# Both LayerNorms of a node unit moved to ScalarE, its steps placed at other points of the block loop, and another order of the node blocks

## What is computed

```python
msg = relu(h[src] + e) + 1e-7
m = msg * t
ex = exp(m - segment_max(m, dst)[dst])
alpha = ex / (segment_sum(ex, dst)[dst] + 1e-16)
agg = segment_sum(msg * alpha, dst)
z = relu(layernorm((h + agg) @ w1 + b1, g1, bb1))   # 128 wide
out = z @ w2 + b2
# from layer 1 on:  h = h + genconv(relu(layernorm(h, ln_g, ln_b)))   # 64 wide
```

## Time and profile before

| | |
|---|---|
| median of 3 runs | 5808.66 us (5808.57 to 5826.21) |
| the profiled execution | 5825.41 us, its span 5823.0 us |
| busy | PE 81%, DVE 78%, ACT 34%, POOL 69% of the span |
| mean granted TensorE clock | 0.868 of full speed |
| layers 0, 1, 2, 3 begin at (first gather) | 1686.0, 2708.5, 3732.3, 4757.7 us |

### The profile page before, as it was taken

One profiled execution on the slowest core, in us unless ns is written; L12 is line 12 of the kernel. 1 busy time (PEld: TensorE's weight loads), 2 busy tenths in 40 slices (PEclk: granted clock), 3 DMA queues, 4 the chain that ended last, 5 costly groups with the idle time before them and its releaser, 6 DMA issues.

```text
span 5823.0 us, 108077 instructions
## 1 busy us (share of the span) xinstructions
PE 4692.3 (81%) x43853; PEld 3246.1 (56%) x43853; DVE 4557.1 (78%) x8649; ACT 1992.2 (34%) x3506; POOL 4032.3 (69%) x3659
## 2 busy tenths in 40 slices
PE   6727788899958888886888798688888867896887
PEld 6726677788945554553555455355545544554544
DVE  9723555654549998996999899699989968997887
ACT  3314675665523332332233223223323322222222
POOL 2433777777637777774777777477777747777775
PEclk8966987976659999998999999899999978998988
DMA  8993777775665556554555655455565545555552
GB/s 338 413 304 111 274 282 270 263 274 211 240 218 196 183 198 181 186 200 144 181 186 200 174 192 193 148 173 198 191 174 200 184 148 177 188 189 161 177 178 96
DMA packets 317390, 1192.47 MB, mean 205 GB/s; under 512 B 139314, under 2 KB 142564, under 8 KB 249556
## 3 DMA queue, kind: packets, MB, share of 16 engines
q1 hardware_dynamic: 166676, 920.68, 42.9%
q0 software_dynamic: 128800, 209.18, 14.0%
q10 hardware_dynamic: 21408, 55.60, 2.4%
HBM read 930.35 MB, written 254.82 MB: 204 GB/s over the span
## 4 chain that ended last, share of the span: by engine, by line
DVE 35%; PE 13%; POOL 10%; issue 8%; DMA 2%; ACT 2%; SPq 0%; DVEq 0%; POOLq 0%
POOL gb L1285 9%; PE bank L1394 9%; DVE ep_layers L1384 5%; DVE xb L1318 5%; DVE ep_layers L1345 5%; DVE ep_layers L1370 4%; DVE ep_layers L1340 4%; PE bank L1302 2%; DMA gb<-ztab,ovi 2%; DVE xb L1328 1%; DVE ds L1404 1%; DVE na L1431 1%; ACT hb L282 1%; DVE st L254 1%; PE bank L1448 1%
## 5 line engine op out<-in xcount | busy, mean ns | idle before, releaser
L1285 POOL DMA_INDIRECT gb<-ztab,ovi x2512 | 2794.2, 1112 | 869.5 <-issue 736.3
L1394 PE MATMUL bank<-ep_layers,keep 128*128 128x512 f32 (+3 forms) x4928 | 2248.6, 616 | 43.2 <-DVE ep_layers L1384 43.2
L1394 PEld LDWEIGHTS bank<-ep_layers,keep 128*128 128x128 f32 x4928 | 995.9, 205 | 1241.1 <-issue 1181.8
L1302 PE MATMUL bank<-zpw,oh_layers 128*128 128x64 bf16 x28812 | 880.8, 194 | 104.2 <-DMA zpw<-ztab 104.1
L1302 PEld LDWEIGHTS bank<-zpw,oh_layers 128*128 128x128 bf16 x28812 | 874.4, 98 | 159.0 <-issue 137.1
L1131 POOL DMA_INDIRECT ecell<-zpw,ptg x588 | 627.3, 1067 | 227.8 <-issue 175.6
L1376 ACT ACTIVATE ep_layers<-ep_layers,pack 128x1280 f32<-128x1280 f32 (+14 forms) x484 | 641.9, 1347 | 190.1 <-DVE ep_layers L1370 183.9
L1370 DVE SCALAR_TENSOR_TENSOR ep_layers<-xb,bank 128x1280 f32<-128x1280 f32 (+14 forms) x484 | 689.2, 1468 | 6.8
L1384 DVE SCALAR_TENSOR_TENSOR ep_layers<-xb,ep_layers 128x1280 f32<-128x1280 f32 (+14 forms) x484 | 687.0, 1469 | 0.4
L960 PE MATMUL bank<-byk,zpw 96*102 96x102 f32 (+13 forms) x4608 | 624.3, 317 | 43.2 <-DVE zpw L941 39.4
L960 PEld LDWEIGHTS bank<-byk,zpw 96*102 96x102 f32 (+13 forms) x4608 | 609.4, 224 | 58.5 <-DVE zpw L941 49.2
(11 more groups left out here) (219 smaller groups left out, 4697.2 us busy)
## 6 DMA issues: line engine op xcount, KB each, us to landing
oh_layers<-ohd SPq DMA_DIRECT2D x196, 1568.0 KB
cb<-rowc SPq DMA_DIRECT2D x49, 1152.0 KB
ea_in<-in_ea SPq DMA_DIRECT2D x101, 512.0 KB, 9.3
enc<-es_out ACTq DMA_DIRECT2D x101, 512.0 KB
gb<-ztab,ovi POOLq DMA_INDIRECT x2512
ohd<-oh_lay SPq DMA_DIRECT2D x49, 736.0 KB
xb<-ecell SPq DMA_DIRECT2D x20, 1536.0 KB
xb<-ecell SPq DMA_DIRECT2D x20, 1504.0 KB
```

Source lines behind the costliest of these rows:

```text
L1285: at["g"][d] = ga_l[d % GB_BLOCKS](GP.indirect_dma_start(gb[:, c:c + 64], None, from_rows, bass.IndirectOffsetOnAxis(ap=ovi[:, i:i + 1], a ...
L1302: q = PE.matmul(gps[j % n_gp][:, 64 * (s % 8):64 * (s % 8) + 64], oh[:, d % 2, at_oh:at_oh + 128], zp[:, b, 64 * part:64 * part + 64], sta ...
L1394: q = PE.matmul(both[:, 0:w], ident, rows[:, 128 * (c - a):128 * (c - a) + w], start=(c == 0), stop=(c + 4 >= S.S[d]), skip_group_check=True)
```

## The change

Four things change.

1. `scalar_norm()` takes the place of `norm()` for both norms of a unit. All of it runs on ACT: sums by activations with an accumulator output, Ln and Exp, a Newton step out of Square and Identity activations, and the scaling. For the first norm `w1` and `b1` have their mean over the 128 outputs taken off once per layer (in `first_of_pack`), so that no mean is needed there; the second norm takes it.
2. `steps` becomes `run_to(part)`, and the pieces stand at other places: in E the transposes and `yt` come after the second `add`, "linear2" after the last one, and `h` and the second norm after `mul`; in O the affine and what follows come after `over`, and the whole first norm comes after `mul`.
3. At the end of a layer the last but one unit is finished before `fold(48)`, not after it.
4. `S.sorted`: four blocks with few gathers stand at places 0 to 3 and five at places 44 to 48; the block with 36 gathers is at place 25. The calculation of the sorted place of a node goes, and `srt` is read with five DMAs.

`V` by place, after: 7, 6, 6, 5, 13, 16, 13, 15, 13, 15, 12, 15, 12, 15, 12, 14, 12, 14, 12, 14, 11, 14, 11, 13, 11 (place 24), 36, 11, 21, 11, 20, 10, 19, 10, 18, 10, 18, 10, 17, 9, 17, 9, 16, 9, 16, 9, 8, 8, 8, 7.

```diff
-        self.turn = self.ND // 2
-        ends = [d // 2 if d % 2 else self.ND - 1 - d // 2 for d in range(self.ND)]
-        self.sorted = ends[self.turn:] + ends[:self.turn]
+        few, half = self.ND - 8, (self.ND - 9) // 2
+        self.runs = [(0, 1, few + 4, 4), (4, 2, half, few - half), (5, 2, half // 2, half - half // 2),
+                     (5 + 2 * (half - half // 2), 2, 0, half // 2), (self.ND - 4, 1, few, 4)]
...
+        def scalar_norm(A, src, width, centred, out):
+
+            total, less, square, root, half, by, fix, shift = (nwf[:, i, :] for i in range(8))
+            if not centred:
+                for s in (0, 1):
+                    q = A(AE.activation(out[:, s, 0:width], src[:, s, 0:width], ACT.Identity,
+                                        accum_out=total[:, s:s + 1]))
+                AE.wait_ge(ae_s, q)
+                q = A(AE.activation(less, total, ACT.Identity, scale=-1.0 / width))
+                AE.wait_ge(ae_s, q)
+            for s in (0, 1):
+                q = A(AE.activation(out[:, s, 0:width], src[:, s, 0:width], ACT.Square,
+                                    bias=0.0 if centred else less[:, s:s + 1],
+                                    accum_out=square[:, s:s + 1]))
+            AE.wait_ge(ae_s, q)
+            q = A(AE.activation(by, square, ACT.Ln, scale=1.0 / width, bias=eps[:, 0:1]))
+            A(AE.activation(half, square, ACT.Identity, scale=-0.5 / width, bias=eps[:, 1:2]))
+            AE.wait_ge(ae_s, q)
+            q = A(AE.activation(root, by, ACT.Exp, scale=-0.5))
+            AE.wait_ge(ae_s, q)
+            q = A(AE.activation(by, root, ACT.Square))
+            AE.wait_ge(ae_s, q)
+            for s in (0, 1):
+                q = A(AE.activation(fix[:, s:s + 1], by[:, s:s + 1], ACT.Identity,
+                                    scale=half[:, s:s + 1], bias=eps[:, 2:3]))
...
+            if not centred:
+                for s in (0, 1):
+                    q = A(AE.activation(shift[:, s:s + 1], less[:, s:s + 1], ACT.Identity,
+                                        scale=root[:, s:s + 1]))
...
                 yield "linear1"
-                VE.wait_ge(pe_s, q)
-                q = yield from norm(V, A, NA[:, 0:256].rearrange("p (s c) -> p s c", s=2),
-                                    128, hb)
+                AE.wait_ge(pe_s, q)
+                q = scalar_norm(A, NA[:, 0:256].rearrange("p (s c) -> p s c", s=2), 128, True, hb)
                 yield "normed"
...
-                yield "turned"
                 AE.wait_ge(pe_s, q)
                 q = A(AE.activation(yt[:, :, :], NB[:, 0:256].rearrange(
                     "p (s c) -> p s c", s=2), ACT.Relu, bias=bb1, scale=g1))
+                yield "turned"
...
-                q = yield from norm(V, A, h[:, u, :].rearrange("p (s f) -> p s f", s=2), 64,
-                                    hb)
-                yield "gap"
+                AE.wait_ge(ve_s, q)
+                q = scalar_norm(A, h[:, u, :].rearrange("p (s f) -> p s f", s=2), 64, False, hb)
+                yield "normed2"
...
                 for j in range(JS):
                     add(d, j)
                     if d + 1 < ND:
                         passes(d + 1, j)
-                    steps(2, "normed")
+                    if not ready and j == 1:
+                        run_to("turned")
+                if not ready:
+                    run_to("linear2")
...
-                steps(2, "normed")
+                if ready:
+                    run_to("rows0")
                 for _ in most(d):
-                    steps(1, "normed")
-                ready = d and S.where[d - 1][0] != S.where[d][0]
-                n = len(slices(d))
-                if ready:
-                    sub(d, 0)
-                steps(99, "end" if ready else "turned")
-                for i in range(1 if ready else 0, n):
+                    if ready:
+                        run_to("rows1")
+                for i in range(n):
                     sub(d, i)
-                steps(99, "linear2")
+                    if i == 0 and ready:
+                        run_to("end")
...
                 for i in range(n):
                     mul(d, i)
-                    if i == n - 1:
-                        steps(4, "normed")
+                run_to("normed" if ready else "normed2")
...
-            fold(ND - 1)
-            steps(99, "end")
+            run_to("end")
             for u in k["node", "rows"]:
                 if u not in zs_at:
                     store_rows(u)
+            fold(ND - 1)
```

More of the change, by code:

```diff
@@ L62, in __init__ @@
         assert self.ones[-1] == self.ND and self.G == 36
-        self.turn = self.ND // 2
-        ends = [d // 2 if d % 2 else self.ND - 1 - d // 2 for d in range(self.ND)]
-        self.sorted = ends[self.turn:] + ends[:self.turn]
+        few, half = self.ND - 8, (self.ND - 9) // 2
+        self.runs = [(0, 1, few + 4, 4), (4, 2, half, few - half), (5, 2, half // 2, half - half // 2),
+                     (5 + 2 * (half - half // 2), 2, 0, half // 2), (self.ND - 4, 1, few, 4)]
+        at = {p + step * i: b + i for p, step, b, n in self.runs for i in range(n)}
+        self.sorted = [at[d] for d in range(self.ND)]
+        assert sorted(self.sorted) == list(range(self.ND))
         self.place = [self.sorted.index(b) for b in range(self.ND)]
@@ L283, in norm @@
                                     bias=shift[:, s:s + 1], scale=root[:, s:s + 1]))
+            return q
+        eps = sb("eps", [128, 3])
+        for i, value in enumerate((LN_EPS, -0.5 * LN_EPS, 1.5)):
+            VE.memset(eps[:, i:i + 1], value)
+        def scalar_norm(A, src, width, centred, out):
[22 more added lines that the diff above has]
+                                    scale=half[:, s:s + 1], bias=eps[:, 2:3]))
+            AE.wait_ge(ae_s, q)
+            for s in (0, 1):
+                q = A(AE.activation(root[:, s:s + 1], root[:, s:s + 1], ACT.Identity,
+                                    scale=fix[:, s:s + 1]))
+            AE.wait_ge(ae_s, q)
+            if not centred:
+                for s in (0, 1):
+                    q = A(AE.activation(shift[:, s:s + 1], less[:, s:s + 1], ACT.Identity,
+                                        scale=root[:, s:s + 1]))
+                AE.wait_ge(ae_s, q)
+            for s in (0, 1):
+                q = A(AE.activation(out[:, s, 0:width], src[:, s, 0:width], ACT.Identity,
+                                    bias=0.0 if centred else shift[:, s:s + 1],
+                                    scale=root[:, s:s + 1]))
@@ L1435, in node_unit @@
                                        ALU.mult))
-                yield
                 vwait(q)
@@ L1514, in node_unit @@
                     if part < 2:
-                        yield "gap"
+                        yield f"rows{part}"
                         VE.wait_ge(ae_s, q)
@@ L1530, in layer, with run_to @@
             now = {"unit": None, "part": None}
-            def steps(n, last):
-                for _ in range(n):
-                    if now["unit"] and now["part"] != last:
-                        part = next(now["unit"], "end")
-                        if part == "gap":
-                            if n < 99:
-                                return
-                            continue
-                        now["part"] = part or now["part"]
-                        if part == "end":
-                            now["unit"] = None
+            def run_to(part):
+                while now["unit"] and now["part"] != part:
+                    now["part"] = next(now["unit"], "end")
+                    if now["part"] == "end":
+                        now["unit"] = None
             def load_pack():
@@ L1550, in first_of_pack @@
                 awaits(VE, got_p)
+                for t in (w1, b1):
+                    t = t.rearrange("p (s c) -> p s c", s=2)
+                    q = V(VE.tensor_reduce(st[:, :, 0], t, AX.X, ALU.add))
+                    vwait(q)
+                    q = V(VE.tensor_scalar(st[:, :, 1], st[:, :, 0], -1.0 / 128, None, ALU.mult))
+                    vwait(q)
+                    for i in (0, 1):
+                        k_c = V(VE.tensor_scalar(t[:, i, :], t[:, i, :], st[:, i, 1:2], None,
+                                                 ALU.add))
+                    vwait(k_c)
+                PE.wait_ge(ve_s, k_c)
                 k_nt = V(VE.tensor_scalar(nt[:, :], tcol, -1.0, None, ALU.mult))
@@ L1591, in layer @@
                     fetch_out(d // 2)
+                ready = d and S.where[d - 1][0] != S.where[d][0]
+                n = len(slices(d))
                 for j in range(JS):
@@ L1620, in layer @@
                     now.update(unit=node_unit(S.where[d - 1][0]), part=None)
-                    steps(99, "linear1")
+                    run_to("linear1")
                 for i in range(n):
                     mul(d, i)
-                    if i == n - 1:
```

(2 more changed lines are left out.)

36 lines of the change are left out of this document (5 added, 31 removed).

## The result

| | before | after |
|---|---|---|
| median | 5811.20 us of 4 runs (5808.57 to 5826.21) | 6050.72 us of 4 runs (6040.96 to 6058.39) |
| ratio after to before | | 1.0406, 95% interval 1.0381 to 1.0430 |
| profiled execution | 5825.41 us | 6040.96 us |
| layers begin at (first gather) | 1686.0, 2708.5, 3732.3, 4757.7 | 1671.1, 2766.0, 3844.6, 4924.5 |

What follows compares the result with a forecast made beforehand. No single bound: DVE, POOL and nearly PE ran at the same rate; afterwards a chain through PE, ACT and DVE. Layers 0 to 2 at +74 each and layer 3 at +28 gave +250, 6058 us on the median's scale, range 5950 to 6150.

Steps and rivals of the forecast that it cites:

- preparation: Before the layers: one load becomes five and a few DVE instructions go, within a few us.
- first half and start: Ten pairs at +1.7 us plus 4 for larger O, less 10 for gather waits gone at the start: +11 a layer.
- middle: `over(24)` to `over(26)`: the 36 gathers now wait for `over(24)`, 82 us instead of 47.0, +35 a layer.
- second half: `over(26)` to `over(48)`, eleven pairs: 463 us instead of 430.7, +33 a layer.
- end: After `over(48)`: -4 at `fold(48)`, -4 from the earlier last but one unit, about 3 for longer norms: -5 a layer.
- layer 3: 98 more POOL instructions make `over(48)` late already; the chain would give 1049 us against 1016.0: +33 - 5 = +28.
- ACT's side, E: In E, `yt` waits behind O's sums and stands ahead of the exponentials, so `mul` is delayed 2.1 us.
- ACT's side, next O: Second norm on ACT alone, 5.1 us (4.5 to 6.1); DVE waits 1.3 us, a pair is 1.7 us longer.
- Size of O: Each slot of O puts 0.40 us on the chain: +4 us at places 5 to 23, +14 at 27 to 47.
- The clock falls too: Rival, chance 0.15: PE idles longer, sums of O go from 12.2 to 13.5 us; 6210 us in all.
- POOL binds: Rival, chance 0.14: exponentials not held up, POOL's 1.44 us an instruction sets the rate; 5855 us in all.
- Faster: Rival, chance 0.07: thinner DVE work cuts POOL's mean instruction from 1.44 to 1.36 us; 5640 us in all.

Runs made afterwards that it cites:

- e3: The kernel after with `yt` and linear2 put back behind the exponentials of E, norms still on ACT: 5942.12 us, ratio 1.0221 to before.
- e4: The kernel after with a second norm that leaves out subtracting the mean (five ACT instructions, two accumulator reads fewer): 5980.62 us, ratio 1.0300 to before.
- e5: The kernel after with place 24's gathers put at the ring's end, so the 36 gathers may start after `over(23)`: 6011.58 us, ratio 1.0337 to before.
- e9: The kernel before with 36 gathers at place 4, small O, large E, larger last blocks, last but one unit finished before `fold(48)`: 5767.57 us, ratio 0.9913.
- e2: The kernel before with the new order of blocks alone, old norms in their old places: 5969.27 us, ratio 1.0270 to before.
- e11: The kernel before with ACT norms and the unit's new places, old order, but `yt` and linear2 behind the exponentials: 5781.00 us, ratio 0.9948.
- e7: The kernel after with ring room for the 36 gathers, small O in the second half, `yt` and linear2 behind the exponentials: 5866.34 us, ratio 1.0082 to before.
- e10: e9's order with the norms on ACT and `yt` and linear2 behind the exponentials: 5752.36 us, ratio 0.9899 to before.

## Why the prediction was right, and where its terms were off

The forecast was +250 us from its profile, and the profile has +215.5 (6040.96 - 5825.41); the medians have +239.5. By the steps, for layer 1 where the layer is one of the first three:

| step | forecast | measured |
|---|---|---|
| preparation | within a few us | -15.0 |
| first half and start | +11 | -6.7 (layer 1), +10.3 (layer 0) |
| middle | +35 | +34.4 |
| second half | +33 | +31.1 |
| end | -5 | -4.2 |
| layers 0, 1, 2 | +74 each | +72.5, +54.7, +54.6 |
| layer 3 | +28 | +48.6 |

The main waits were the ones forecast. That the sum came so near is in part luck: the first three layers have +181.8 where 222 was forecast, and layer 3 has 48.6 where 28 was.

**ACT's side, E: right.** `mul` waits 2.17 us, 2.1 forecast, for the reason given; e3 removes it, and 108.6 us with it. That is nearly as much as the middle, which has +123.6 us over the four layers of the profile. That `yt` stands ahead of the exponentials is what makes the norms on ACT look slow.

**ACT's side, next O: right.** The second norm takes 5.0 us (5.1), the wait for `hb` is 1.34 (1.3), and the pair is longer by 1.56 (1.7); e4, with the norm at 3.3 us, shows that its length counts. The first norm, 2130.27 to 2133.60, is 3.3 us (3.6). By the rule of the Trainium skill (ScalarE: Activation LUTs, What ACT_TABLE_LOAD costs) the estimate was 4.6 us for the second norm; the trace has 5.0, and it decides. The rule fits the one-column instruction of the Newton step, an estimate of 186 + 0.8 + 2 x 93 = 373 ns against 379 measured. The estimate counted no reads of the accumulator, of which this norm has four (last section).

**Middle: right**, and the cause too: `over(24)` to `over(25)` is 55.5 us (56), e5 moves the start of the gathers and the wait shrinks, e9 puts them elsewhere and the stall in the middle is gone.

**Size of O: mis-assigned.** It was taken as a term of the chain with the new norms, +14 us in the second half. e2 shows +24 in the second half of layer 1 with the old norms, against the kernel before, whose O blocks have 92 slots less there (482, now 574): 0.26 us a slot. 17.4 of the 24 are the wait of the addition to `h` in its eleven pairs, and most of the rest is the 6.9 us of `zb` waiting for a store. The pair term there, +19, was too high in turn: of the 31.1, 23.7 are there in e2, and the norms and `yt` add 7.4. (The forecast's 14 stand for 35 slots over 49 each, so they can't be set against the 24 one to one.) That the sum of the second half came out (+31) although its split did not is luck.

**First half and start: off by 18 us in layers 1 and 2.** The start gained 16 us, not 10 (`over(4)` 81.4 us after the first gather, before 97.6). And +1.7 a pair was worked out from one pair of layer 0; in layer 1 the ten pairs from `over(4)` to `over(24)` went from 39.6 to 40.5 us, +0.9 each. In layer 0, where the pairs before were shorter (38.9 us), it is +1.6 each, and the start gains 5.7 us only, so the sum is right there.

**Layer 3: off by 21 us the other way.** I took the later of two delays, the chain's and POOL's. But they nearly add: before, `over(48)` came 44.5 us later behind its first gather in layer 3 than in layer 1, and after it still comes 37.0 us later. Measured against before, the first half is +2.4, the middle +20.4 (83.4 against 63.1), the second half +28.6 and the end -2.8. Before, POOL held `over(48)` (last gather at 1009.9, `over(48)` at 1016.0); after, 1017.2 and 1067.3, and the end is not POOL's. The second half alone takes 485 us, in layer 1 462.5; what lengthens the pairs of layer 3 with POOL's 98 instructions more was not tried apart.

**Preparation.** It differs from execution to execution and not with the change: layer 0 begins at 1665.3 to 1695.2 us in the thirteen profiles. It is 15 of the 24 us by which the profile's 215.5 lie below the medians' 239.5.

**The rivals.** *The clock falls too*: the granted clock is 0.92 in the stretch where it was 0.94, a mean near the upper of its two levels (2.4 GHz), and O's 26 sums take 12.56 us for 50 slots (those from 2089.20 on), 12.35 for 49 before, not 13.5. It is 0.87 in the window that has the stall of the middle, which is priced by its own length already. From 1680 us to the end it is 0.88, before 0.91, but PE is busy 3405.0 us there, before 3399.3: the clock is lower, and in PE's busy time it costs next to nothing. *POOL binds*: it idles in the steady stretch. It comes true where `yt` is out of the way: in the same window POOL is full in e11 (297.51 + 252 x 0.3 = 373 us), e7, e9 and e10, and nearly in e3 (365). *Faster*: its mechanism was a shorter POOL instruction, and a gather takes 1124 ns on average after, 1112 before. But the norms on ACT do gain once `yt` doesn't stand in the way (e11), which the prediction did not consider.

## What to carry to other kernels

Work moved to an idle engine brings its place in that engine's queue with it: `yt`, 0.56 us long, cost 108.6 us where it stood (e3), because it waited for another engine ahead of what the full engine wanted next. Look at what stands behind the waiting instruction before counting the work that is saved. When an order of blocks is chosen, ask three things of each block: which engine is full there, whether its transfers have enough time of their engine ahead of them, and whether the last blocks still give every full engine something to do.

## What the runs showed of the hardware

An activation with an accumulator output is followed by an instruction of its own, also on ACT. From the first sum of the second norm in the kernel after:

```profile
2109.79 0.26 ACT L298 ACTIVATE hb<-h 128x64 f32<-128x64 f32 x1 [2.27 <-DVE h L1495]
2109.96 0.19 ACT L298 ACTIVATION_READ_ACCUMULATOR hb<-h 128x1 f32 x1
...
2110.41 0.20 ACT L301 ACTIVATE nwf<-nwf 128x2 f32<-128x2 f32 x1
```

Two such sums of 64 columns take 0.62 us in all, up to the start of the next instruction (2109.79 to 2110.41), and the second norm has four. A Newton step out of one-column activations with two operands per partition is dear for what it does:

```profile
L316 ACT ACTIVATE nwf<-nwf,eps 128x1 f32<-128x1 f32 x400 | 132.9, 379 | 6.7
```

379 ns each for one column, more than the 0.28 us that 128 columns without such operands take in the first norm:

```profile
2089.45 0.28 ACT L304 ACTIVATE hb<-bank 128x128 f32<-128x128 f32 x1 [2.17 <-PE bank L1475]
```
